# Layer 2 attention: softmax rows scaled on GpSimd ahead of the transposes, with scores two tiles ahead, in place of a widened and transposed reciprocal

## The chip, the cores and the metric

The kernel runs on one core of a Trainium2 chip. It is a chain of four transformer-like layers in one program. The metric is the device time of one execution in microseconds (us), taken as the median of several. Four engines do the computing: TensorE (PE in the rows, its weight loads PEld), VectorE (DVE), ScalarE (ACT) and GpSimd (POOL). Each engine works through its own instructions in order; they wait for each other by semaphores. TensorE writes its results into PSUM, which has eight banks of 128 partitions x 512 float32.

## The reference, cut to what matters

Only the attention of layer 2 is touched. It is called with 8 sequences of 512 rows, 128 wide, and has 16 heads of 64:

```python
q = split_heads(inputs @ Wq)
k = split_heads(inputs @ Wk)
v = split_heads(inputs @ Wv)
scores = jnp.einsum('bnqd,bnkd->bnqk', q, k) + position_bias
attn = jax.nn.softmax(scores, axis=-1)
hidden = jnp.einsum('bnqk,bnkd->bnqd', attn, v)
return hidden @ Wo
```

So each row of exponents must be divided by its sum somewhere between the exponential and the output product.

## The kernel before

`t5_attention_block` works through STEPS = 64 steps, one for each sequence (8) and pair of heads (8). A step n has four tiles t of 128 query rows, and each tile two heads h: eight units of 128 x 512 values. In this text the parts of a step on TensorE have letters:

- **Q, K, V**: the products of the pair (`q_product`, `k_product` into a bank each; `v_product`, four tiles of rows, into the bank of Q). DVE cuts q and k into a high and a low part (`cut_q`, `low_q`, `cut_k`, `low_k`), ACT copies the high ones (`high_q`, `high_k`) and v (`store_v`).
- **S(n,t)** (`scores`, L1690): for a tile, three products for each head, six matmuls of 64 rows, into two PSUM banks, one for each head. There are just these two, so S of the next tile waits for `biased` of this one.
- DVE then adds the bias from the table `skewed` and takes the row's extreme (`bias`, L1868), writing a unit of the ring `p`; ACT raises it in place and sums it (`exponents`, L1797), by `accum_out` into `sums`.
- **T(n,t)** (`turns`, a helper at L129): eight 128 x 128 transposes of the two units of p. DVE and ACT copy one head's result each to `pT` (`move`, L1877 and L1805; the buffer's name is `t_pT` or `g`).
- **M** (`mix`, L1712), in two halves of four matmuls: v times the turned exponents of the step before, a head in each half of the output columns.
- **W** (`turn_scale`, L129): DVE inverts the eight columns of sums of a step (`invert`, L1884), Pool spreads each over 64 columns into `wide` (L1947), PE turns it (four transposes) into the bank of K, ACT copies it to `scale` (L1812), and DVE multiplies the mixed heads by it (`norm`, L1891) into `hT`.
- **O** (`output`, L1727): `wo` times hT, summed over the eight pairs of a sequence in one bank. Once a sequence, `turn_sum` turns the sum back (four transposes; `sum_out` and `store_sum` on DVE).

TensorE's order in a step, written out by hand in the loop over n, is: S(n,1), T0, Q(n+1), K(n+1), S(n,2), T1, first half of M(n-1), S(n,3), T2, second half of M(n-1), S(n+1,0), T3, O(n-2), W(n-1), V(n+1). Scores are thus one tile ahead of the transposes (`after`). The ring p has RING = 4 units. Pool also issues, in the first 32 steps, two indirect DMAs a step (`scatter`, L624), which have nothing to do with the attention but stand behind its instruction on Pool's queue; SP only loads weights of later layers.

Of the kernel before, what the change touches and what calls it, by code (L numbers as in the profile page):

```python
# [19 lines left out]
ALU = mybir.AluOpType  # L20
# [1591 lines left out]
def t5_attention_block(k, wq, wk, wv, wo, skewed, loads, late_loads):  # L1612

    nc, NB = k.nc, k.NB
    PAIRS, HALF, RING = HEADS // 2, P // 2, 4
    STEPS = NB * PAIRS
    with ExitStack() as ctx:
# [9 lines left out]
        wide, scale = st.sb("wide", [P, 8, HALF]), st.sb("scale", [P, SEQ])  # L1627
# [7 lines left out]
        mixed, inverted, widened = st.sem("mixed"), st.sem("inverted"), st.sem("widened")  # L1635
        scale_made, scaled, normed = st.sem("scale_made"), st.sem("scaled"), st.sem("normed")
# [10 lines left out]
        def after(n, t):  # L1647

            return (n, t + 1) if t + 1 < TPS else (n + 1, 0)

        @block.tensor
        def _(pe):
# [7 lines left out]
            def k_product(n):  # L1660
                if n >= 3:
                    pe.wait_ge(scaled, n - 2)
                elif n >= 1:
                    pe.wait_ge(k_low, n)
# [30 lines left out]
            def turns(n, t):  # L1695
                for h in range(2):
                    u = unit(n, t, h)
                    pe.wait_ge(expd, u + 1)
# [17 lines left out]

            def turn_scale(n):
                pe.wait_ge(widened, n + 1)
                pe.wait_ge(k_low, min(n + 3, STEPS))
                turn(nc, kc_ps, [wide[:, 2 * t:2 * t + 2, :].rearrange("p a c -> p (a c)") for t in range(TPS)],  # L1720
                     k.ident).then_inc(scale_made, 1)
# [19 lines left out]
            scores(0, 0)  # L1741
            for n in range(STEPS + 2):
                live = n < STEPS
                if live:
                    scores(n, 1)
                    turns(n, 0)
                if n + 1 < STEPS:
                    q_product(n + 1)
                    k_product(n + 1)
                if live:  # L1750
                    scores(n, 2)
                    turns(n, 1)
# [703 lines left out]
```

## Time and profile before

| what | value |
|---|---|
| median of 3 runs | 2474.96 us (2468.89 to 2475.29) |
| profiled execution, its own time | 2463.91 us |
| its span | 2462.2 us |
| TensorE busy over the span | 2040.5 us (83%) |
| DVE, ACT, POOL busy over the span | 1458.4, 1179.5, 443.8 us |
| the stage in question | from 756.5 to 1751.2 us of the span, 994.7 us |

Rows of a timeline have the start in us, the time from the first start to the last end of what is merged in the row, the engine, the source line, the operation, output <- input, and xN for N instructions merged. TensorE's instructions overlap, so its steps are read from start to start. A float32 matmul of 512 columns is two instructions in the trace (x2), a transpose one. What stands in brackets is idle time of that engine just before, and what ended it. A row of busy times has the stretch, its length, then the busy time of PE, PEld, DVE, ACT and POOL with their instructions, TensorE's granted clock (1.00 is full speed), the busy share of the DMA engines and GB/s.

### The profile page before, as it was taken

The numbers are of one execution on the slowest core, as the hardware profiler recorded it, in microseconds if no ns is written. First come the engines' busy times: TensorE is split into PE (matmuls) and PEld (weight loads), VectorE is DVE, ScalarE is ACT, GpSimd is POOL, SyncE is SP. The second block draws the span as 40 slices with busy tenths as digits, with TensorE's granted clock in tenths as the row PEclk, the third lists the DMA queues.
The fourth block names the chain that finished last, engine by engine and source line by source line (L and its number), as shares of the span: only waits on it lengthen the run. The fifth ranks groups of instructions, "written<-read, shape, count | busy, mean of one in ns | idle before, by whom it ended". The sixth has DMA issues, their size and how long they took to land. (4 is left out here: it accounts for less than half of the span.)

```text
span 2462.2 us, 41326 instructions
## 1 busy us (share of the span) xinstructions
PE 2040.5 (83%) x14039; PEld 1319.4 (54%) x14039; DVE 1458.4 (59%) x4086; ACT 1179.5 (48%) x2380; POOL 443.8 (18%) x522
## 2 busy tenths in 40 slices
PE   3435998468759999999999999999796188989978
PEld 3223996347744555555555555555596034444447
DVE  4675223642166777777777777777464766666615
ACT  1122553234436666666666666666232205555563
POOL 0154551044410111111110000000065100000000
PEclk9866998768959999999999999999898558898899
DMA  3412662045460000000000000001175322322101
GB/s 128 130 41 92 230 228 81 9 136 179 153 172 20 10 10 10 10 10 10 10 6 1 1 1 1 1 1 53 61 254 175 102 71 83 104 66 76 51 4 35
DMA packets 120234, 173.06 MB, mean 70 GB/s; under 512 B 16136, under 2 KB 79344, under 8 KB 119584
## 3 DMA queue, kind: packets, MB, share of 16 engines
q1 hardware_dynamic: 108016, 141.38, 18.2%
q0 software_dynamic: 11584, 23.91, 2.8%
q10 hardware_dynamic: 432, 5.19, 0.5%
q8 instruction: 113, 1.85, 0.3%
q14 instruction: 89, 0.73, 0.1%
HBM read 68.27 MB, written 45.40 MB: 46 GB/s over the span
## 5 line engine op out<-in xcount | busy, mean ns | idle before, releaser
L1797 ACT ACTIVATE t_p<-t_p,t_low 128x512 f32<-128x512 f32 x512 | 369.3, 721 | 333.4 <-DVE t_low L1868 333.3
L1868 DVE CUSTOM_DVE_ANT_0 t_p<-bank,L_skewed 128x512 f32<-128x512 f32 x512 | 332.6, 687 | 276.8 <-PE bank L1690 276.8
L129 PE MATMUL pair<-ident,t_p 128*128 128x128 f32 x2048 | 279.9, 280 | 0.0
L129 PEld LDWEIGHTS pair<-ident,t_p 128*128 128x128 f32 x2048 | 219.0, 141 | 94.8 <-issue 92.6
L2205 ACT ACTIVATE alibi_p<-pair 128x1024 f32<-128x1024 f32 (+1 forms) x192 | 169.0, 884 | 164.6 <-PE pair L2092 164.4
L2264 DVE CUSTOM_DVE_ANT_0 alibi_junk<-bank,alibi_later 128x512 bf16<-128x512 f32 (+1 forms) x256 | 150.8, 623 | 95.2 <-PE bank L2104 92.8
L1947 POOL COPY t_wide<-t_inverse 128x512 f32<-128x512 f32 x64 | 39.1, 611 | 892.2 <-DVE t_inverse L1884 883.4
L2104 PE MATMUL bank<-alibi_k_aug,alibi_q_aug 32*128 32x512 f32 (+1 forms) x256 | 105.3, 559 | 36.7 <-DMA alibi_k_aug<-aug_k 16.8
L1690 PEld LDWEIGHTS bank<-t_k_hi,t_q_hi 64*128 64x128 f32 x512 | 47.7, 183 | 161.6 <-issue 149.6
L1690 PE MATMUL bank<-t_k_hi,t_q_hi 64*128 64x512 f32 x512 | 127.8, 496 | 3.5 <-DVE t_low L1868 3.2
L1712 PE MATMUL pair<-t_pT,t_v 128*64 128x512 f32 x512 | 123.8, 605 | 1.6 <-DVE t_hT L1891 1.6
L1712 PE MATMUL pair<-g,t_v 128*64 128x512 f32 x512 | 124.0, 605 | 0.0
L2151 PE MATMUL bank<-alibi_p,alibi_v_aug 128*32 128x512 f32 (+3 forms) x1024 | 100.2, 490 | 15.6 <-ACT g L2211 15.6
L1690 PE MATMUL bank<-t_k_lo,t_q_hi 64*128 64x512 f32 x512 | 101.7, 394 | 0.0
L1690 PE MATMUL bank<-t_k_hi,t_q_lo 64*128 64x512 f32 x512 | 100.8, 390 | 0.0
L1797 ACT ACTIVATION_READ_ACCUMULATOR t_p<-t_p,t_low 128x1 f32 x512 | 96.3, 188 | 0.0
L2080 PE MATMUL pair<-alibi_q_aug,alibi_k_aug 32*128 32x384 f32 (+3 forms) x512 | 95.6, 412 | 0.3 <-ACT alibi_p L2205 0.2
L742 PEld LDWEIGHTS pair<-L0moe_w,L0moe_hT 128*128 128x128 f32 x624 | 91.9, 193 | 6.3
L742 PE MATMUL pair<-L0moe_w,L0moe_hT 128*128 128x128 f32 x624 | 95.2, 276 | 0.0
L703 POOL DMA_INDIRECT answers<-L0moe_y,L0moe_at x78 | 75.5, 967 | 81.9 <-DVE L0moe_at L803 68.3
L1877 DVE COPY t_pT<-pair 128x512 f32<-128x512 f32 x128 | 87.8, 686 | 1.6 <-PE pair L129 1.6
L2080 PEld LDWEIGHTS pair<-alibi_q_aug,alibi_k_aug 32*128 32x128 f32 x512 | 49.2, 201 | 72.6 <-issue 37.3
(488 smaller groups left out, 4401.6 us busy)
## 6 DMA issues: line engine op xcount, KB each, us to landing
L0moe_w<-L_packed SPq DMA_DIRECT2D x39, 578.0 KB, 3.4
L2moe_w<-L_skewed SPq DMA_DIRECT2D x39, 450.0 KB, 3.1
L1moe_w<-L_packed SPq DMA_DIRECT2D x23, 578.0 KB, 3.4
alibi_q_aug<-aug_q SPq DMA_DIRECT2D x8, 1024.0 KB, 7.6
alibi_k_aug<-aug_k SPq DMA_DIRECT2D x8, 1024.0 KB, 8.1
L_skewed<-bias_table SPq DMA_DIRECT2D x16, 448.0 KB, 10.3
slots<-g ACTq DMA_DIRECT2D x3, 1690.0 KB, 11.9
L0moe_xs<-slots SPq DMA_DIRECT2D x39, 130.0 KB, 3.2
```

Of the source, the lines that this page charges most:

```text
L129: last = nc.tensor.transpose(out[0:piece.shape[1], j * P:j * P + piece.shape[0]], piece, ident[0:piece.shape[0], 0:piece.shape[0]])
L742: ins = nc.tensor.matmul(down_ps[i % 2][:, h * P:(h + 1) * P], hT[:, n % (2 * chunks), h * P:(h + 1) * P], w[:, i % DEEP, at:at + P], star ...
L1690: ins = nc.tensor.matmul(score_ps[h][:], left[rows[h], n % 2, tile], right[rows[h], n % 2, :], start=(j == 0), stop=(j == 2))
L1712: ins = nc.tensor.matmul(mix_ps[rows[h], :], v[:, n % 2, j, rows[h]], pT[n % 2][:, h, j, :], start=(j == 0), stop=(j == TPS - 1))
L1797: nc.scalar.activation(p[:, u % RING, :], p[:, u % RING, :], ACT.Exp, bias=low[:, u % 16:u % 16 + 1], scale=-1.0, accum_out=sums[:, n % 2, ...
L1868: nc.vector.tensor_tensor_reduce(out=p[:, u % RING, :], in0=score_ps[h][:], in1=skewed[:, (n % PAIRS) * 2 + h, start:start + SEQ], scale=- ...
L1877: nc.vector.tensor_copy(pT[n % 2][:, 0, :, t * P:(t + 1) * P], turn_ps[0][:].rearrange("p (j n) -> p j n", n=P)).then_inc(moved[0], 1)
L2080: nc.tensor.matmul(flip_ps[u % 2][:, r % 2, a:e], k_aug[rows(r), n % AUG, G, c * P:(c + 1) * P], q_aug[rows(r), n % AUG, G, c * P:SEQ], st ...
L2104: nc.tensor.matmul(bank[:, 0:w], q_aug[rows(r), b % AUG, G, t * P:w], k_aug[rows(r), b % AUG, G, 0:w], start=True, stop=True).then_inc(sco ...
L2151: ins = nc.tensor.matmul(mix_ps[rows(r), c * P:SEQ], v_aug[:, n % 2, c, 4 * G + r, :], p[:, slot, r % 2, a:e], start=(c == 0), stop=True, ...
L2205: nc.scalar.activation(p[:, u % P_RING, :, 0:w], flip_ps[u % 2][:, :, 0:w], ACT.Exp).then_inc(expd, 1)
L2264: nc.vector.tensor_tensor_reduce(out=junk[:, s % 2, 0:w], in0=score_ps[s % 2][:, 0:w], in1=later[:, SEQ - w:SEQ], scale=1.0, scalar=-HUGE, ...
```

## The change

Pool now multiplies every unit of p in place by one over its row sums, between the exponential and the transposes. DVE inverts two columns of sums a tile in place of eight a step. W, the widened tile, `scale`, its copy on ACT and the multiplication on DVE are gone; what is left of `norm` is a plain copy from PSUM to hT, on ACT. Transposes wait for `divided` in place of `expd`. To leave room for this the scores run two tiles ahead of the transposes, p has 6 units, and the orders on PE, ACT and DVE are written anew. The diff, cut to its core:

```diff
-    PAIRS, HALF, RING = HEADS // 2, P // 2, 4
+    PAIRS, HALF, RING = HEADS // 2, P // 2, 6
...
-            return (n, t + 1) if t + 1 < TPS else (n + 1, 0)
+            return (n, t + 2) if t + 2 < TPS else (n + 1, t + 2 - TPS)
...
             def k_product(n):
-                if n >= 3:
-                    pe.wait_ge(scaled, n - 2)
-                elif n >= 1:
+                if n >= 1:
                     pe.wait_ge(k_low, n)
...
-                    pe.wait_ge(expd, u + 1)
+                    pe.wait_ge(divided, u + 1)
...
-            def turn_scale(n):
-                pe.wait_ge(widened, n + 1)
-                pe.wait_ge(k_low, min(n + 3, STEPS))
-                turn(nc, kc_ps, [wide[:, 2 * t:2 * t + 2, :].rearrange("p a c -> p (a c)") for t in range(TPS)],
-                     k.ident).then_inc(scale_made, 1)
...
+            k_product(1)
+            scores(0, 1)
             for n in range(STEPS + 2):
-                live = n < STEPS
-                if live:
-                    scores(n, 1)
-                    turns(n, 0)
-                if n + 1 < STEPS:
-                    q_product(n + 1)
-                    k_product(n + 1)
+                live, more = n < STEPS, n + 1 < STEPS
                 if live:
                     scores(n, 2)
+                    turns(n, 0)
+                if more:
+                    q_product(n + 1)
+                if live:
+                    scores(n, 3)
                     turns(n, 1)
                 if 1 <= n <= STEPS:
                     mix(n - 1, 0)
                 if live:
-                    scores(n, 3)
                     turns(n, 2)
+                if 1 <= n <= STEPS:
+                    mix(n - 1, 1)
                 if n % PAIRS == 2 and n >= PAIRS and n < STEPS:
                     turn_sum(n // PAIRS - 1)
-                if 1 <= n <= STEPS:
-                    mix(n - 1, 1)
-                if n + 1 < STEPS:
+                if more:
                     scores(n + 1, 0)
                 if live:
                     turns(n, 3)
                 if n >= 2:
                     output(n - 2)
-                if 1 <= n <= STEPS:
-                    turn_scale(n - 1)
-                if n + 1 < STEPS:
+                if more:
+                    scores(n + 1, 1)
                     v_product(n + 1)
+                if n + 2 < STEPS:
+                    k_product(n + 2)
...
-            def store_scale(n):
-                act.wait_ge(scale_made, n + 1)
+            def norm(n):
+                act.wait_ge(mixed, n + 1)
                 if n >= 1:
-                    act.wait_ge(normed, n)
-                nc.scalar.copy(scale[:], kc_ps[:]).then_inc(scaled, 1)
+                    act.wait_ge(added, n)
+                nc.scalar.copy(hT[:], mix_ps[:]).then_inc(normed, 1)
...
-            def invert(n):
-                dve.wait_ge(expd, (n + 1) * 8)
+            def invert(n, t):
+                dve.wait_ge(expd, unit(n, t, 1) + 1)
                 if n >= 2:
-                    dve.wait_ge(widened, n - 1)
-                nc.vector.reciprocal(inverse[:, n % 2, :], sums[:, n % 2, :]).then_inc(inverted, 1)
-
-            def norm(n):
-                dve.wait_ge(mixed, n + 1)
-                dve.wait_ge(scaled, n + 1)
-                if n >= 1:
-                    dve.wait_ge(added, n)
-                nc.vector.tensor_tensor(hT[:], mix_ps[:], scale[:], ALU.mult).then_inc(normed, 1)
+                    dve.wait_ge(divided, unit(n - 1, 0, 0))
+                nc.vector.reciprocal(inverse[:, n % 2, 2 * t:2 * t + 2], sums[:, n % 2, 2 * t:2 * t + 2]).then_inc(inverted, 1)
...
         @block.gpsimd
-                pool.wait_ge(inverted, n + 1)
-                if n >= 1:
-                    pool.wait_ge(scale_made, n)
-                nc.gpsimd.tensor_copy(wide[:], inverse[:, n % 2, :].unsqueeze(2).to_broadcast([P, 8, HALF])).then_inc(widened, 1)
+                for t in range(TPS):
+                    for h in range(2):
+                        u = unit(n, t, h)
+                        pool.wait_ge(inverted, n * TPS + t + 1)
+                        nc.gpsimd.tensor_scalar(p[:, u % RING, :], p[:, u % RING, :], inverse[:, n % 2, t * 2 + h:t * 2 + h + 1],
+                                                None, ALU.mult).then_inc(divided, 1)
```

ACT's order in a step is now, with E for an exponential and its tile of step n: E(2) of head 0, move(0), E(2) of head 1, norm(n-2), high_k(n+1); E(3), move(1), E(3), high_q(n+1); move(2), E and E of tile 0 of step n+1; move(3), E and E of tile 1 of step n+1, store_v(n+1).

TensorE at the end of a step, before; the rows are T(n,3), O, W, V, then S(n+1,1) in three rows and T(n+1,0):

```order
L129 MATMUL pair<-ident,t_p 128x128 x8
L1727 MATMUL pair<-t_hT,L_wo 128x512
L129 MATMUL bank<-ident,t_wide 128x128 x4
L1676 MATMUL bank<-L_wv,xnT 128x128 x4
L1690 MATMUL bank<-t_k_hi,t_q_hi 128x512 x2
L1690 MATMUL bank<-t_k_lo,t_q_hi 128x512 x2
L1690 MATMUL bank<-t_k_hi,t_q_lo 128x512 x2
L129 MATMUL pair<-ident,t_p 128x128 x8
```

The same place now (S is L1686, V L1672, K L1663, O L1717):

```order
L129 MATMUL pair<-ident,t_p 128x128 x8
L1717 MATMUL pair<-t_hT,L_wo 128x512
L1686 MATMUL bank<-t_k_hi,t_q_hi 128x512 x2
L1686 MATMUL bank<-t_k_lo,t_q_hi 128x512 x2
L1686 MATMUL bank<-t_k_hi,t_q_lo 128x512 x2
L1672 MATMUL bank<-L_wv,xnT 128x128 x4
L1663 MATMUL bank<-xnT,L_wk 128x512
```

W is gone, S(n+1,1) stands ahead of V, and K has come here from its place beside Q.

DVE at the start of a step, before. The two rows `ISA` are one `bias`, its main part and the read of its accumulator; then come `move`, the reciprocal, q's two parts and `norm`:

```order
L1868 ISA t_p,t_low<-bank,L_skewed 128x512
L1868 ISA t_low 128x1
L1877 COPY t_pT<-pair 128x4x128
L1884 RECIPROCAL t_inverse<-t_sums 128x8
L1842 TENSOR_SCALAR t_q_cut<-bank 128x512
L1849 TENSOR_TENSOR t_q_lo<-bank,t_q_cut 128x512
L1891 TENSOR_TENSOR t_hT<-pair,t_scale 128x512
L1868 ISA t_p,t_low<-bank,L_skewed 128x512
```

And now, from the reciprocal of tile 1 to that of tile 2:

```order
L1880 RECIPROCAL t_inverse<-t_sums 128x2
L1864 ISA t_p,t_low<-bank,L_skewed 128x512
L1864 ISA t_low 128x1
L1864 ISA t_p,t_low<-bank,L_skewed 128x512
L1864 ISA t_low 128x1
L1873 COPY g<-pair 128x4x128
L1851 TENSOR_SCALAR t_k_cut<-bank 128x512
L1856 TENSOR_TENSOR t_k_lo<-bank,t_k_cut 128x512
L1880 RECIPROCAL t_inverse<-t_sums 128x2
```

A reciprocal, which waits for ACT's exponentials, now stands ahead of each pair of `bias` instructions (or, in the second half of a step, ahead of the `move` in front of them), and `norm` has left the engine.

## Rows read from the trace of the kernel before

**Rows 1.** Busy time of the engines in the stage of layer 2's attention

```profile
756.50:1751.20 994.70, 985.97 (x5792) 560.44 (x5792) 701.17 (x1680) 646.10 (x1536) 101.52 (x128) 1.00 0.03 10
```

**Rows 2.** TensorE's largest wait from 756 to 1745 us: total, times, longest

```profile
PE bank L1690 <- DVE t_low L1868: 3.2, 4, 1.4
```

**Rows 3.** Timeline of TensorE through one step: W, V, S, T, Q, K, S, T, M, S, O, W

```profile
1203.09 0.60 PE L129 MATMUL bank<-ident,t_wide 128*128 128x128 f32 x4
1203.53 1.06 PE L1676 MATMUL bank<-L_wv,xnT 128*128 128x128 f32 x8
1204.51 0.51 PE L1690 MATMUL bank<-t_k_hi,t_q_hi 64*128 64x512 f32 x2
...
1205.42 1.09 PE L129 MATMUL pair<-ident,t_p 128*128 128x128 f32 x8
1206.35 1.02 PE L1658 MATMUL bank<-xnT,L_wq 128*128 128x512 f32 x2
1207.21 1.02 PE L1667 MATMUL bank<-xnT,L_wk 128*128 128x512 f32 x2
1208.16 0.50 PE L1690 MATMUL bank<-t_k_hi,t_q_hi 64*128 64x512 f32 x2
...
1209.05 1.09 PE L129 MATMUL pair<-ident,t_p 128*128 128x128 f32 x8
1210.08 1.94 PE L1712 MATMUL pair<-g,t_v 128*64 128x512 f32 x8
1211.94 0.50 PE L1690 MATMUL bank<-t_k_hi,t_q_hi 64*128 64x512 f32 x2
...
1217.55 1.02 PE L1727 MATMUL pair<-t_hT,L_wo 128*128 128x512 f32 x2
1218.41 0.60 PE L129 MATMUL bank<-ident,t_wide 128*128 128x128 f32 x4
```

**Rows 4.** Timeline at the stage's start, where the engines wait for each other

```profile
761.59 0.69 DVE L1868 CUSTOM_DVE_ANT_0 t_p<-bank,L_skewed 128x512 f32<-128x512 f32 x1 [1.15 <-PE bank L1690]
...
762.21 0.69 DVE L1868 CUSTOM_DVE_ANT_0 t_p<-bank,L_skewed 128x512 f32<-128x512 f32 x1
762.33 0.72 ACT L1797 ACTIVATE t_p<-t_p,t_low 128x512 f32<-128x512 f32 x1 [1.37 <-DVE t_low L1868]
...
762.96 0.19 ACT L1797 ACTIVATION_READ_ACCUMULATOR t_p<-t_p,t_low 128x1 f32 x1
...
762.96 0.50 PE L1690 MATMUL bank<-t_k_hi,t_q_hi 64*128 64x512 f32 x2 [1.38 <-DVE t_low L1868]
763.05 0.71 ACT L1797 ACTIVATE t_p<-t_p,t_low 128x512 f32<-128x512 f32 x1
...
763.97 0.69 DVE L1868 CUSTOM_DVE_ANT_0 t_p<-bank,L_skewed 128x512 f32<-128x512 f32 x1 [1.06 <-PE bank L1690]
```

**Rows 5.** Timeline of the reciprocal and of Pool in the same step

```profile
1207.35 0.19 DVE L1884 RECIPROCAL t_inverse<-t_sums 128x8 f32<-128x8 f32 x1
...
1207.46 0.64 DVE L1842 TENSOR_SCALAR t_q_cut<-bank 128x512 int32<-128x512 int32 x1
...
1207.61 0.61 POOL L1947 COPY t_wide<-t_inverse 128x512 f32<-128x512 f32 x1 [12.31 <-DVE t_inverse L1884]
...
1208.38 0.97 POOL L624 DMA_INDIRECT slots<-s,slot  x1 [0.16 <-issue]
```

**Rows 6.** Timeline in layer 3, where Pool and DVE work at once

```profile
2088.87 1.28 POOL L2352 TENSOR_TENSOR alibi_lo<-alibi_full,alibi_hi 128x512 f32<-128x512 f32 x1 [3.85 <-DVE alibi_hi L2300]
...
2089.15 0.69 DVE L2264 CUSTOM_DVE_ANT_0 alibi_junk<-bank,alibi_later 128x512 bf16<-128x512 f32 x1 [0.36 <-PE bank L2104]
```

**Rows 7.** Timeline at the stage's end: the last M, O, W, and O

```profile
1741.29 3.65 PE L1712 MATMUL pair<-t_pT,t_v 128*64 128x512 f32 x16 [1.55 <-DVE t_hT L1891]
...
1744.87 1.13 PE L1727 MATMUL pair<-t_hT,L_wo 128*128 128x512 f32 x2
...
1747.89 1.13 PE L1727 MATMUL pair<-t_hT,L_wo 128*128 128x512 f32 x2 [1.46 <-DVE t_hT L1891]
```

More of the change, by code:

```diff
@@ L1626, in t5_attention_block @@
         low, sums, inverse = st.sb("low", [P, 16]), st.sb("sums", [P, 2, 8]), st.sb("inverse", [P, 2, 8])
-        wide, scale = st.sb("wide", [P, 8, HALF]), st.sb("scale", [P, SEQ])
         hT, sT = st.sb("hT", [P, SEQ]), st.sb("sT", [P, SEQ])
@@ L1634, in t5_attention_block @@
         moved = [st.sem("moved0"), st.sem("moved1")]
-        mixed, inverted, widened = st.sem("mixed"), st.sem("inverted"), st.sem("widened")
-        scale_made, scaled, normed = st.sem("scale_made"), st.sem("scaled"), st.sem("normed")
+        mixed, inverted, divided, normed = st.sem("mixed"), st.sem("inverted"), st.sem("divided"), st.sem("normed")
         sent = st.sem("sent")
@@ L1795, in exponents @@
                 if t == 0 and h == 0 and n >= 2:
-                    act.wait_ge(inverted, n - 1)
+                    act.wait_ge(inverted, (n - 1) * TPS)
                 nc.scalar.activation(p[:, u % RING, :], p[:, u % RING, :], ACT.Exp, bias=low[:, u % 16:u % 16 + 1], scale=-1.0,
@@ L1816, in _ @@
             store_v(0)
-            exponents(0, 0, 0)
-            exponents(0, 0, 1)
-            for n in range(STEPS + 1):
+            for t in range(2):
+                exponents(0, t, 0)
+                exponents(0, t, 1)
+            for n in range(STEPS + 2):
                 for t in range(TPS):
@@ L1822, in _ @@
                         m, s = after(n, t)
+                        if t >= 2:
+                            move(n, t)
                         if m < STEPS:
                             exponents(m, s, 0)
-                        move(n, t)
+                        if t < 2:
+                            move(n, t)
                         if m < STEPS:
                             exponents(m, s, 1)
+                    if t == 0 and n >= 2:
+                        norm(n - 2)
+                    if t == 0 and n + 1 < STEPS:
+                        high_k(n + 1)
                     if t == 1 and n + 1 < STEPS:
                         high_q(n + 1)
-                        high_k(n + 1)
-                    if t == 3 and n >= 1:
-                        store_scale(n - 1)
                     if t == 3 and n + 1 < STEPS:
@@ L1907, in _ @@
             low_k(0)
-            bias(0, 0, 0)
-            bias(0, 0, 1)
-            for n in range(STEPS + 2):
-                for t in range(TPS):
-                    if n < STEPS:
-                        m, s = after(n, t)
-                        if m < STEPS:
-                            bias(m, s, 0)
-                            bias(m, s, 1)
-                        move(n, t)
-                    if t == 0 and 1 <= n <= STEPS:
-                        invert(n - 1)
+            for t in range(2):
+                bias(0, t, 0)
+                bias(0, t, 1)
+            invert(0, 0)
+            for n in range(STEPS):
+                for t in range(TPS):
+                    m, s = after(n, t)
+                    if t + 1 < TPS:
+                        invert(n, t + 1)
+                    elif n + 1 < STEPS:
+                        invert(n + 1, 0)
+                    if t >= 2:
+                        move(n, t)
+                    if m < STEPS:
+                        bias(m, s, 0)
+                        bias(m, s, 1)
+                    if t < 2:
+                        move(n, t)
                     if t == 0 and n + 1 < STEPS:
+                        cut_k(n + 1)
+                        low_k(n + 1)
+                    if t == 1 and n + 1 < STEPS:
                         cut_q(n + 1)
                         low_q(n + 1)
-                    if t == 0 and n >= 2:
-                        norm(n - 2)
-                    if t == 1 and n + 1 < STEPS:
-                        cut_k(n + 1)
-                        low_k(n + 1)
                     if t == 1 and n % PAIRS == 2 and PAIRS <= n < STEPS:
```

## The prediction, made before the changed kernel ran

> **What bounds the kernel now.** I read the stage's busy times first. In the 994.7 us of layer 2's attention TensorE counts 985.97 us as busy, at a granted clock of 1.00 (its 2.4 GHz level), DVE 701 us, ACT 646 us, Pool 102 us [rows 1]. A busy PE is not PE at its peak, so I then read its waits: over the whole stage the largest sum is 3.2 us, in four waits for DVE at the start [rows 2], and there is one of 1.55 us ahead of the last M [rows 7]. Between those, no semaphore holds it. So a step lasts as long as TensorE's own list, and the third view says how long that is: from W to W it is 1218.41 - 1203.09 = 15.32 us [rows 3]. Read from start to start, its parts are W 0.44, V 0.98, S 0.91, T 0.93 ahead of Q, Q 0.86, K 0.95 ahead of S, T 1.03 ahead of M, half of M 1.86, O 0.86 [rows 3]. The three parts of the step left out of the rows (two S with T, one M) repeat these within 0.02.
>
> The same rows show a cost that belongs to an order and not to an operation: Q followed by K takes 0.86, K followed by S 0.95; T ahead of Q 0.93, ahead of M 1.03 [rows 3]. Going between whole-array matmuls and the half-array ones (S in rows, M in columns) costs 0.09 or 0.10 us.
>
> **The change on TensorE.** Removed: W, 0.44 a step. Moved: S(n+1,1) stands behind O, and S(n,3) behind Q. O costs 0.86 ahead of W and Q 0.86 ahead of K; each is now followed by S, which I price like K ahead of S, 0.95: +0.09 twice. V now leads into K and not into S; by its eight instructions at W's pace (four in 0.44) it should take between 0.88 and 0.98, I take 0.92: -0.06. K ahead of S stays. One half of M now leads into T and not into S; both are changes of the array's division, so I leave it at 1.86. S ahead of V I price like S ahead of T, no difference. Sum: -0.44 + 0.09 + 0.09 - 0.06 = -0.32, a step of 15.00 us. The bounds from rows are -0.26 (V stays at 0.98) and -0.44 (no cost for the new borders).
>
> **The change on the other engines**, and whether it fits under 15.00. Put time 0 at S(n,2). TensorE, if nothing holds it: T0 0.90, Q 1.83, S(n,3) 2.78, T1 3.68, M 4.7, T2 6.57, M 7.6, S(n+1,0) 9.5, T3 10.4, O 11.3, S(n+1,1) 12.25, V 13.15, K 14.1, S(n+1,2) 15.0. What the engines need between each other I take from the start of the stage, where they do wait:
> - S start to bias of head 0: 763.97 - 762.96 = 1.01; bias to bias 762.21 - 761.59 = 0.62; second bias to the next S 762.96 - 762.21 = 0.75 [rows 4].
> - bias to its exponential 0.74; exponential to exponential 0.72; the sum is out at 762.96 + 0.19, 0.82 after the exponential's start, so about 0.88 until DVE can go on [rows 4].
> - reciprocal to the next DVE instruction 0.11, reciprocal to Pool's start 0.26, Pool's copy of 512 columns to its next instruction 0.77 [rows 5].
>
> **The tightest chain** runs from S(n+1,0) to S(n+1,2). Its bias ends only after 1.01 + 0.74 + 0.72 + 0.88 have brought the second exponential's sum to DVE: there the new reciprocal stands in the queue ahead of the move and of the bias of tile 1, and S(n+1,2) is behind that bias. 1.01 + 0.74 + 0.72 + 0.88 + 0.11 (reciprocal) + 0.62 (move) + 0.62 + 0.75 = 5.45 us. TensorE's list between the two is 15.0 - 9.5 = 5.5. It fits with some 0.1 to spare. The other reciprocals have more room: that of tile 2 comes at 4.15 (behind cut_k and low_k), delays the bias of tile 3 to 4.3, and the next S needs that only at 9.5. DVE's work itself is a wash: norm, as wide as a bias (0.69, rows 4), against three more reciprocals of 0.19 [rows 5]. So is ACT's: a copy of PSUM for a copy of PSUM, and at 4.2 it frees M at 4.7.
>
> **Pool's multiplication** has no row. From below it is bounded by the copy of the same width, one input, 0.61 long and 0.77 to the next [rows 5]; from above by the two-input subtraction of 128x512, 1.28 [rows 6], with the same 0.16 behind it 1.44. It reads one tensor, so I take it near the copy: 0.65, 0.8 from one to the next. For tile 2, the one with least time, Pool starts at 4.15 + 0.26 = 4.4; heads are done at 5.1 and 5.9, and T2 wants them at 6.57 and 7.03. At 1.44 the second is done at 7.13 plus a semaphore: up to 0.2 late. The scatter's two DMAs (0.97 each, some 2.5 us together) stand behind tile 3's multiplications: Pool is free of them at about 7.7 + 1.6 + 2.5 = 11.8, and tile 0's reciprocal comes at 12.8. Eight multiplications at 0.8 are 6.4 us of 15. All of this is hidden at 0.8; if that cover went, each 0.1 us by which T is late costs 6.4 us in all.
>
> **The ends.** At the start, K and V of the next step stand in front of T and Pool adds its latency to the first ones: I put +1 us. At the end, the last M waited 1.55 us for hT, and the last O came at 1747.89, 3.0 us after the M made way for the O ahead of it at 1744.87, through W, the scale's copy and norm [rows 7]. Now the M needs only a plain copy that stands right behind the last move, so I take that wait as gone; and from M to the last O there is one ACT copy beside the O ahead of it (0.86), some 0.9 in place of 3.0: -3.7. Together -2.7.
>
> **Sum.** 63 steps x -0.32 = -20.2, with the ends -22.9 us. The profiled execution took 2463.91, so it would be 2441.0; the median of the runs shown is 11 us above that execution, and the same difference gives 2474.96 - 22.9 = 2452. By the bounds: -0.26 a step gives 2456, -0.44 (where the DVE chain of 5.45 would bind too, within 0.1) 2445 or a little less; Pool at 1.44 gives back 0.2 a step, 2465.
>
> **Rivals.**
> 1. *Part of the gain goes to new waits* (0.17). Either Pool costs nearly what the two-input row says, or the chain of 5.45 is longer than I add up by 0.1 to 0.3, since it has only 0.1 to spare: 0.2 a step given back is 2465, 0.3 is 2471. For it speaks that this chain crosses four engines and that in the kernel before DVE's bias never stood behind ACT's sums. Against it: every link has a row.
> 2. *Pool and DVE block each other* (0.10), the case on the slower side. Pool reads and writes 512 columns eight times a step while DVE runs. If in the tight chain one DVE instruction had to wait out one multiplication, 0.65 more would make it 6.1 against TensorE's 5.5: +0.55 a step, less 0.32, is +14 us, with the ends 2487; two such blocks would make it 2528. It turns slower than before once the chain is some 0.45 longer. Against it: in layer 3, Pool's subtraction (1.28, two reads) overlaps a DVE instruction of just the kind of `bias`, one input in PSUM, one in SBUF, and that takes the 0.69 that it takes alone [rows 4, 6].
>    The Trainium skill, "SBUF — State Buffer", in the rules on the port pair that DVE and GpSimd share, has this very rule: whichever starts first holds the pair for its whole instruction when the DVE instruction is in a 2-port mode or has two SBUF inputs. By its other half, an instruction with at most one SBUF input does not contend, this chain's DVE work would be free of it, and the trace agrees (0.69 in both places).
> 3. *Nothing is gained* (0.03): W filled time in which TensorE would have waited anyway. Its few microseconds of waits in the whole stage [rows 2, 7] leave no room for that. 2472.
>
> **How the numbers follow.** Forecast 0.70, 2452 us, its own range 2442 to 2459. A measurement of this kernel can tell about 0.3% (7.4 us) from no change, so faster is below 2467.5: the forecast and 0.12 of rival 1, 0.82. Within 0.3%: 0.05 of rival 1 and rival 3, 0.08. Slower: rival 2, 0.10. The range runs from 2441 (no cost for the new borders, and the spread of the runs) to 2468, which takes in Pool's upper bound and leaves out rival 2 and the worse part of rival 1.
>
> **What the profile would show.** TensorE's list from S to S at 15.0 us with next to no waits; Q and O ahead of S at 0.95, V ahead of K near 0.92. Pool's rows at 0.6 to 0.8 us, 512 of them; if they are at 1.3, T waits for Pool by up to 0.2. S(n+1,2) waiting for DVE a step means that the chain of 5.45 is mis-added. A bias that takes more than 0.69 while Pool runs means rival 2. An end of the stage with under 1 us between the last M and the last O. I am wrong if TensorE shows a wait in every step, wherever it is.

## The result, and the profile after

The changed kernel takes 2501.57 us, the median of 4 runs (2497.41 to 2503.7), against 2475.12 us (4 runs, 2468.89 to 2475.99) for the kernel before beside it: a ratio of 1.0126, 95% interval 1.0106 to 1.0145. It is slower by 26.5 us, where 23 us less were forecast. The profiled execution took 2500.13 us.

First the page of the changed kernel, its costliest groups: line, engine, operation, output <- input, count | busy us, mean ns of one | idle time before, and what ended it.

```profile
L1941 POOL TENSOR_SCALAR t_p<-t_p,t_inverse 128x512 f32<-128x512 f32 x512 | 793.1, 1562 | 163.5 <-DVE t_inverse L1880 157.9
...
L1864 DVE CUSTOM_DVE_ANT_0 t_p<-bank,L_skewed 128x512 f32<-128x512 f32 x512 | 331.4, 685 | 197.9 <-PE bank L1686 197.9
L129 PE MATMUL pair<-ident,t_p 128*128 128x128 f32 x2048 | 299.1, 283 | 22.3 <-POOL t_p L1941 21.1
L129 PEld LDWEIGHTS pair<-ident,t_p 128*128 128x128 f32 x2048 | 217.0, 141 | 165.8 <-POOL t_p L1941 110.8
```

Pool's multiplication takes 1562 ns, not 650. And TensorE's transposes, which had no wait worth a row [rows 2], now have one, for Pool. The waits of TensorE over the same 756 to 1745 us as [rows 2], total, times, longest:

```profile
PE pair L129 <- POOL t_p L1941: 20.3, 64, 0.9
PE bank L1686 <- DVE t_low L1864: 2.1, 3, 1.4
```

64 times in 20.3 us is about once a step, 0.32 us in the mean. Where in the step, the timeline of TensorE shows; these rows answer to [rows 3] (S is L1686, Q L1656, M L1708, O L1717, V L1672, K L1663):

```profile
1002.25 0.50 PE L1686 MATMUL bank<-t_k_hi,t_q_hi 64*128 64x512 f32 x2
...
1003.14 1.09 PE L129 MATMUL pair<-ident,t_p 128*128 128x128 f32 x8
1004.07 1.02 PE L1656 MATMUL bank<-xnT,L_wq 128*128 128x512 f32 x2
1005.02 0.50 PE L1686 MATMUL bank<-t_k_hi,t_q_hi 64*128 64x512 f32 x2
...
1005.92 1.16 PE L129 MATMUL pair<-ident,t_p 128*128 128x128 f32 x8
1007.01 1.94 PE L1708 MATMUL pair<-g,t_v 128*64 128x512 f32 x8
1008.88 0.66 PE L129 MATMUL pair<-ident,t_p 128*128 128x128 f32 x4
1009.80 0.66 PE L129 MATMUL pair<-ident,t_p 128*128 128x128 f32 x4 [0.27 <-POOL t_p L1941]
1010.39 1.94 PE L1708 MATMUL pair<-g,t_v 128*64 128x512 f32 x8
1012.26 0.50 PE L1686 MATMUL bank<-t_k_hi,t_q_hi 64*128 64x512 f32 x2
...
1014.08 1.02 PE L1717 MATMUL pair<-t_hT,L_wo 128*128 128x512 f32 x2
1015.04 0.50 PE L1686 MATMUL bank<-t_k_hi,t_q_hi 64*128 64x512 f32 x2
...
1015.93 1.16 PE L1672 MATMUL bank<-L_wv,xnT 128*128 128x128 f32 x8
1016.92 1.02 PE L1663 MATMUL bank<-xnT,L_wk 128*128 128x512 f32 x2
1017.88 0.50 PE L1686 MATMUL bank<-t_k_hi,t_q_hi 64*128 64x512 f32 x2
```

A step is 1017.88 - 1002.25 = 15.63 us (15.64 between other O's), against 15.32 before. T2 is split: from its first head to M it takes 10.39 - 8.88 = 1.51 us, where an undisturbed T takes 1.03 ahead of M [rows 3]. T1 is stretched a little: 1.09 to M. The rest is as forecast within 0.02, save one: V ahead of K takes 0.99, not 0.92. Pool beside it:

```profile
1006.40 0.15 DVE L1880 RECIPROCAL t_inverse<-t_sums 128x2 f32<-128x2 f32 x1
...
1006.65 6.31 POOL L1941 TENSOR_SCALAR t_p<-t_p,t_inverse 128x512 f32<-128x512 f32 x4 [0.28 <-DVE t_inverse L1880]
```

Tile 2's reciprocal comes at 1006.40 and Pool starts 0.25 later, 4.40 us after S(n,2): just the 4.4 of the prediction. Four multiplications, the two of tile 2 and the two of tile 3, then take 6.31 us, (6.31 - 1.56) / 3 = 1.58 from one to the next. The second head's is done at 1006.65 + 1.58 + 1.56 = 1009.79, and the transposes of that head start at 1009.80.

How long the stage is, one row per kernel tells: the instructions of O, with the shortest, median and longest in ns and the first and last start in us. For the kernel before:

```profile
L1727 PE MATMUL pair<-t_hT,L_wo x128: 592/594/697, 802.5 to 1748.4; 128*128 128x512 f32 x128
```

And after:

```profile
L1717 PE MATMUL pair<-t_hT,L_wo x128: 592/594/697, 810.2 to 1775.4; 128*128 128x512 f32 x128
```

The last O comes 27.0 us later, in a stage that began at nearly the same time (756.3 and 756.5): about as much as the 26.5 us between the medians. 7.7 of it are there at the first O. From the last O to the end of the span it is 723.0 us after and 713.8 before; over the kernels of this study this part is 711.4 to 723.0, though nothing in it was changed. It goes with the clock that TensorE was granted there: 0.81 of full speed in the three profiles with 720.6 to 723.0 (the changed kernel, experiments 4 and 5), 0.82 or 0.83 in the nine with 711.4 to 715.9. Why the clock differs is open. Below I therefore compare the last O's as well as the times.

### The profile page after: what moved, and what is told of

It reads as the page before. It is cut to its first block and busy times, and to the rows that moved or that the text cites. A ratio compares the mean times of both kernels' runs of the same rounds, so it can differ in the third digit from the quotient of the medians.

```text
span 2498.4 us, 41381 instructions
## 1 busy us (share of the span) xinstructions
PE 2059.6 (82%) x13783; PEld 1284.0 (51%) x13783; DVE 1440.0 (58%) x4214; ACT 1178.9 (47%) x2380; POOL 1192.7 (48%) x970
## 5 line engine op out<-in xcount | busy, mean ns | idle before, releaser
L1941 POOL TENSOR_SCALAR t_p<-t_p,t_inverse 128x512 f32<-128x512 f32 x512 | 793.1, 1562 | 163.5 <-DVE t_inverse L1880 157.9
L129 PE MATMUL pair<-ident,t_p 128*128 128x128 f32 x2048 | 299.1, 283 | 22.3 <-POOL t_p L1941 21.1
L2347 POOL TENSOR_TENSOR alibi_lo<-alibi_full,alibi_hi 128x512 f32<-128x512 f32 x16 | 20.3, 1270 | 362.3 <-DVE alibi_hi L2295 339.2
L1686 PEld LDWEIGHTS bank<-t_k_hi,t_q_hi 64*128 64x128 f32 x512 | 47.8, 183 | 193.7 <-DVE t_low L1864 144.5
L1686 PE MATMUL bank<-t_k_hi,t_q_hi 64*128 64x512 f32 x512 | 127.8, 496 | 3.6 <-DVE t_low L1864 3.0
L1708 PE MATMUL pair<-t_pT,t_v 128*64 128x512 f32 x512 | 123.8, 605 | 1.1 <-ACT t_hT L1803 1.1
L1708 PE MATMUL pair<-g,t_v 128*64 128x512 f32 x512 | 124.0, 605 | 0.0
L703 POOL DMA_INDIRECT answers<-L0moe_y,L0moe_at x78 | 74.7, 957 | 81.6 <-DVE L0moe_at L803 68.0
L1880 DVE RECIPROCAL t_inverse<-t_sums 128x2 f32<-128x2 f32 x256 | 41.0, 160 | 122.7 <-ACT t_p L1788 122.7
L624 POOL DMA_INDIRECT slots<-L_rows,slot x64 | 65.6, 1026 | 93.3 <-POOLq L1114 47.4
L1686 PE MATMUL bank<-t_k_lo,t_q_hi 64*128 64x512 f32 x512 | 101.3, 392 | 0.0
L1686 PE MATMUL bank<-t_k_hi,t_q_lo 64*128 64x512 f32 x512 | 101.1, 391 | 0.0
L703 POOL DMA_INDIRECT answers<-L2moe_y,L2moe_at x78 | 74.8, 958 | 48.2 <-DVE L2moe_at L803 34.3
```

Of the source, the lines that this page charges most:

```text
L129: last = nc.tensor.transpose(out[0:piece.shape[1], j * P:j * P + piece.shape[0]], piece, ident[0:piece.shape[0], 0:piece.shape[0]])
L703: nc.gpsimd.indirect_dma_start(out=k.answers, out_offset=bass.IndirectOffsetOnAxis(at[:, i % AT_DEEP, h:h + 1], 0), in_=y[:, i % Y_DEEP, h ...
L1686: ins = nc.tensor.matmul(score_ps[h][:], left[rows[h], n % 2, tile], right[rows[h], n % 2, :], start=(j == 0), stop=(j == 2))
L1708: ins = nc.tensor.matmul(mix_ps[rows[h], :], v[:, n % 2, j, rows[h]], pT[n % 2][:, h, j, :], start=(j == 0), stop=(j == TPS - 1))
L1941: nc.gpsimd.tensor_scalar(p[:, u % RING, :], p[:, u % RING, :], inverse[:, n % 2, t * 2 + h:t * 2 + h + 1], None, ALU.mult).then_inc(divid ...
```

## The experiments

Theory A: Pool's multiplication costs 1.56, T2 and T1 come late by that, and nothing else is wrong. Theory B: the new order of TensorE, with its chain of 5.45 us over four engines, costs more than I added up, whatever Pool does. Theory C: Pool and DVE hold each other up.

**1. The new order, without the multiplications.** All eight are left out (so the division by the sums is missing), and T waits for the exponentials:

```diff
-                    pe.wait_ge(divided, u + 1)
+                    pe.wait_ge(expd, u + 1)
...
-                if n >= 2:
-                    dve.wait_ge(divided, unit(n - 1, 0, 0))
...
-                for t in range(TPS):
-                    for h in range(2):
-                        u = unit(n, t, h)
-                        pool.wait_ge(inverted, n * TPS + t + 1)
-                        nc.gpsimd.tensor_scalar(p[:, u % RING, :], p[:, u % RING, :], inverse[:, n % 2, t * 2 + h:t * 2 + h + 1],
-                                                None, ALU.mult).then_inc(divided, 1)
+                pool.wait_ge(inverted, (n + 1) * TPS)
```

> The changed kernel with Pool's multiplications left out (the rows of p are not divided by their sums) and the transposes waiting for the exponentials; orders on all engines as changed. Theory (price): the changed step lasts 15.64 us because one multiplication on Pool costs 1.55 us, so that the second head of tile 2 comes 0.47 us late and the first 0.06. Without it a step is 15.1, the stage some 34 us shorter, about 2467 us. Rival (order): the new order and the reciprocals in DVE's queue cost the time whatever Pool does; then the step stays at 15.5 or more and the time near 2500.

Measured: 2450.57 us (4 runs, 2438.04 to 2454.74), ratio to before 0.9891 (0.9842 to 0.9940); last O at 1733.7. Two O's in a row on its timeline of TensorE:

```profile
1439.51 1.02 PE L1717 MATMUL pair<-t_hT,L_wo 128*128 128x512 f32 x2
...
1454.58 1.02 PE L1717 MATMUL pair<-t_hT,L_wo 128*128 128x512 f32 x2
```

15.07 us a step. The time is some 16 us below the expected 2467: the first O comes 6.7 us sooner than in the changed kernel, and the part behind the last O is 10 us shorter, at the higher clock. The order by itself gains 0.25 and has no wait of its own: over 800 to 1720 us TensorE waits for nothing longer than 0.5 us, twice. Theory B falls. Pool's work is worth 15.64 - 15.07 = 0.57 us a step.

**2. The removal alone.** The kernel before in its old order, without W, its copy and its multiplication (the division is missing here too; `norm` is a plain copy on DVE):

```diff
-                if 1 <= n <= STEPS:
-                    turn_scale(n - 1)
...
-                nc.vector.tensor_tensor(hT[:], mix_ps[:], scale[:], ALU.mult).then_inc(normed, 1)
+                nc.vector.tensor_copy(hT[:], mix_ps[:]).then_inc(normed, 1)
```

> The kernel before with W left out (the four transposes of the widened reciprocals, the copy to scale, and the multiplication by it, so nothing is divided by the sums), norm a plain copy on DVE; all other orders as before. It measures by itself what taking W away is worth on TensorE. Both theories: 0.44 us a step less, or 0.35 if the border between O and V costs something, so 14.9 and about 2445 us. If W had been hidden, no change from 2475.

Measured: 2437.74 us (4 runs), ratio 0.9860 (0.9817 to 0.9903), last O at 1716.3, and a step (from one O to the next, 1441.51 to 1456.39) of 14.88 us. W was worth 15.32 - 14.88 = 0.44, all of it. The old order without W is 0.19 a step shorter than the new one without its multiplications: that is what Q and O ahead of S cost (0.09 each), and 0.01 for V ahead of K.

**3. The same multiplication as another instruction.** Pool multiplies with `tensor_tensor`, the column of 1/sum spread along the row by its access pattern. The result and the order are the same:

```diff
-                        nc.gpsimd.tensor_scalar(p[:, u % RING, :], p[:, u % RING, :], inverse[:, n % 2, t * 2 + h:t * 2 + h + 1],
-                                                None, ALU.mult).then_inc(divided, 1)
+                        row = inverse[:, n % 2, t * 2 + h:t * 2 + h + 1].to_broadcast([P, SEQ])
+                        nc.gpsimd.tensor_tensor(p[:, u % RING, :], p[:, u % RING, :], row, ALU.mult).then_inc(divided, 1)
```

> The changed kernel with Pool multiplying by a tensor-tensor instruction whose second input is the column of the reciprocal, broadcast over 512 columns. Theory (price): that form should cost about 1.27 us like the subtraction in layer 3; two of them are 0.56 us less, more than the 0.47 by which tile 2 is late, so T2 waits no more and the step is 15.1 to 15.2, about 2468 us. If the form costs 1.55 too, or the order is to blame, 2500.

Measured: 2447.42 us (6 runs, 2444.31 to 2463.16), ratio 0.9905 (0.9870 to 0.9939); last O at 1734.1, 0.4 us from that of experiment 1. The first row is from its groups of instructions, the second is all there is of waits of TensorE from 800 to 1720 us:

```profile
L1942 POOL TENSOR_TENSOR t_p<-t_p,t_inverse 128x512 f32<-128x512 f32 x512 | 521.8, 1041 | 394.3 <-DVE t_inverse L1880 394.3
```

```profile
PE bank L1686 <- DVE t_low L1864: 0.9, 2, 0.5
```

At 1.04 us Pool is hidden wholly: from O to O 15.07 us, as without any multiplication. The chain of four engines, the reciprocals and Pool's place in it are all still there, and only the instruction's form is another. That settles A for nearly the whole of the loss: one number of one instruction turned a gain of some 1% into a loss of 1.3%.

**4. The prices on Pool apart.** In the kernel before, from step 36 on where Pool is nearly idle, it runs pairs of multiplications on a tile that nobody uses, each waiting for the one ahead; 8 of each kind.

```diff
+                elif n >= 36:
+                    for _ in range(2):
+                        count[0] += 1
+                        pool.wait_ge(probed, count[0])
+                        probe((n - 36) // 4)
```

> The kernel before, with extra instructions on Pool's queue in steps 36 to 63, where it is idle for 14 us a step: two of a kind in each step, four steps a kind, on a tile of their own of 128x512 float32: multiply by a scalar column, by an immediate, tensor by tensor, tensor by a broadcast column, copy of a broadcast column, and by a scalar column on 256 and on 128 columns. It measures the disputed cost by itself. Theory (price): scalar column 1.55, broadcast column 1.02, tensor by tensor 1.27, copy 0.61, whatever the other engines do; if the 1.55 came from the load of the scalar it would be a constant, and 128 columns would cost over 1 us; if it is the pace, 256 columns cost 0.8 and 128 columns 0.45. Rival (contention with DVE or in place): 1.0 or less here.

Its groups on Pool; `eps` is a column of one value, spread along the row in the `TENSOR_TENSOR` and the `COPY`:

```profile
L1949 POOL TENSOR_SCALAR t_pa<-t_pa,eps 128x512 f32<-128x512 f32 x8 | 12.5, 1566 | 0.4
L1951 POOL TENSOR_SCALAR t_pa<-t_pa 128x512 f32<-128x512 f32 x8 | 11.9, 1489 | 0.3
L1955 POOL TENSOR_TENSOR t_pa<-t_pa,eps 128x512 f32<-128x512 f32 x8 | 8.3, 1040 | 0.3
L1953 POOL TENSOR_TENSOR t_pa<-t_pa 128x512 f32<-128x512 f32 x8 | 8.3, 1040 | 0.3
L1959 POOL TENSOR_SCALAR t_pa<-t_pa,eps 128x256 f32<-128x256 f32 x8 | 7.4, 923 | 0.4
L1957 POOL COPY t_pa<-eps 128x512 f32<-128x512 f32 x8 | 4.9, 614 | 0.2
L1961 POOL TENSOR_SCALAR t_pa<-t_pa,eps 128x128 f32<-128x128 f32 x8 | 4.8, 602 | 0.4
```

Among these it is the operation's kind that sets the price, and not the number of inputs: `tensor_scalar` costs 1.57 with a column, 1.49 with a constant, `tensor_tensor` 1.04, where I had expected 1.27 for two tensors. From 128 to 512 columns it grows by (1566 - 602) / 384 = 2.51 ns a column, with some 0.28 us besides. It costs here what it costs in the changed kernel (1.566 and 1.562). DVE works beside it in both, so this pair by itself does not clear DVE; the trace of the changed kernel does. In the step shown above DVE stands still from 1010.35 to 1013.26, and the multiplication that runs from 1011.40 to 1012.96 takes 1.56 all the same.

**5. Another place for T2.** Both halves of M ahead of T2, which gives T2 1.87 us more of room and saves one border between M and T:

```diff
                 if 1 <= n <= STEPS:
                     mix(n - 1, 0)
+                    mix(n - 1, 1)
                 if live:
                     turns(n, 2)
-                if 1 <= n <= STEPS:
-                    mix(n - 1, 1)
```

> The changed kernel with both halves of M ahead of T2 in TensorE's order, nothing else. Theory (price): T2 comes 1.9 us later and finds its rows ready although Pool still takes 1.55; and two borders between M and T fall away, 0.2 to 0.26 us. A step without scatter is 14.9. In the 32 steps with scatter Pool itself has 8 x 1.55 + 2.7 us and its waits of some 0.3 to 0.7, so 15.1 to 15.7 there. Together about 2465 us (2455 to 2480). Rival (order): no gain beyond the borders, some 2485.

Measured: 2456.97 us (7 runs), ratio 0.9945 (0.9911 to 0.9978), last O at 1740.9. With Pool still at 1.56, steps take 15.06 once the scatters are over (O at 1446.04 and 1461.10), and by turns some 15.06 and 15.21 with them. That is 0.58 a step saved with Pool's price unchanged; 0.15 of it is the border of M that is gone (experiment 6), so the room for T2 gave 0.43. Without the scatters T3 is now the one that Pool makes a little late (1.07 to O in place of 0.93), since its two multiplications stand right behind those of tile 2 on Pool; with them it is T1, 1.16 and 1.28 to M in two steps in a row, in place of 1.03.

**6. Both edits**, 3 and 5, in one kernel.

> The changed kernel with both edits: Pool multiplies by the tensor-tensor form with the broadcast column (1.02 us one, as the run before showed) and both halves of M stand ahead of T2. Theory (price, and borders of TensorE's order): with the cheap form no T waits, 15.07 a step; M in one piece saves the two borders between M and T, 0.26 us by this kernel's rows, so 14.81 a step and some 17 us less than the cheap form alone, about 2431 us. Rival: another wait stands right behind (the chain from S(n+1,0) to S(n+1,2) of 5.45, or T3), and the step stays near 15.0, 2444.

Measured: 2439.33 us (6 runs, 2435.79 to 2446.14), ratio 0.9879 (0.9845 to 0.9913), last O at 1723.0.

```profile
1446.47 1.02 PE L1717 MATMUL pair<-t_hT,L_wo 128*128 128x512 f32 x2
...
1461.39 1.02 PE L1717 MATMUL pair<-t_hT,L_wo 128*128 128x512 f32 x2
```

14.92 us a step, 0.15 under experiment 3: M in one run of 16 takes 3.59 instead of twice 1.87, which saves 0.15, and T ahead of S costs the 1.02 that T ahead of M does; for that reason the step is not the 14.81 that I had expected, for which both borders had to go. This version computes what the reference does and beats both kernels.

**7. Only tile 2 with the cheap form**, to split the 0.57 by tile:

```diff
-                        nc.gpsimd.tensor_scalar(p[:, u % RING, :], p[:, u % RING, :], inverse[:, n % 2, t * 2 + h:t * 2 + h + 1],
-                                                None, ALU.mult).then_inc(divided, 1)
+                        col = inverse[:, n % 2, t * 2 + h:t * 2 + h + 1]
+                        if t == 2:
+                            ins = nc.gpsimd.tensor_tensor(p[:, u % RING, :], p[:, u % RING, :], col.to_broadcast([P, SEQ]), ALU.mult)
+                        else:
+                            ins = nc.gpsimd.tensor_scalar(p[:, u % RING, :], p[:, u % RING, :], col, None, ALU.mult)
+                        ins.then_inc(divided, 1)
```

> The changed kernel with the cheap form (tensor by broadcast column, 1.04 us) for the two units of tile 2 alone; the six others stay at 1.56. It tells tile 2's lateness from Pool's load. Theory (lateness of tile 2): nearly the whole gain of the cheap form comes back, 15.1 a step, about 2450 us. Rival (Pool's load as a whole, with scatter in 32 steps): only the 1.04 us of load goes, so the steps with scatter stay at 15.4 or more, 2465 or more.

Measured: 2464.04 us (10 runs), ratio 0.9972 (0.9953 to 0.9992); last O at 1741.2. Steps take 15.12 without the scatters (1445.29, 1460.41) and by turns some 15.14 and 15.28 with them. Tile 2 is thus 0.52 of the 0.57 where Pool has nothing else to do; with the scatters in front of tile 0, T1 comes late as well (1.23 to M in one step), at 1.56 a multiplication. The time lies between the two that I had expected: lateness of tile 2 is most of the loss, Pool's load a small part in 32 of the steps.

**8. All multiplications on DVE**, where one costs 0.48, to see whether another engine would do better. `divide` stands behind the two `bias` of its quarter of the step:

```diff
...
                     if m < STEPS:
                         bias(m, s, 0)
                         bias(m, s, 1)
+                    if t == 0:
+                        divide(n, 1)
                     if t < 2:
                         move(n, t)
+                    if t == 1:
+                        divide(n, 2)
+                    if t == 2:
+                        divide(n, 3)
+                    if t == 3 and n + 1 < STEPS:
+                        divide(n + 1, 0)
...
```

> The changed kernel with all the multiplications on DVE (a tensor by scalar column, in place, SBUF to SBUF) behind the bias instructions, Pool left with its scatter. Theory (price): DVE should do one in 0.42 us, as it does the cut of 128x512 in SBUF in layer 3, 0.35 to the next, 2.8 us a step on an engine that has 4 us to spare; T2's first head comes some 0.3 us late, so a step of 15.1 to 15.4, 2450 to 2465 us. Rival: DVE becomes the bound, 15.7 or more, 2500.

Measured: 2657.41 us (4 runs), ratio 1.0762 (1.0714 to 1.0809): much slower, against my expectation. Its timeline at one place:

```profile
1400.55 0.69 DVE L1865 CUSTOM_DVE_ANT_0 t_p<-bank,L_skewed 128x512 f32<-128x512 f32 x1 [1.55 <-PE bank L1687]
...
1401.78 0.88 DVE L1888 TENSOR_SCALAR t_p<-t_p,t_inverse 128x512 f32<-128x512 f32 x2
...
1402.32 1.09 PE L129 MATMUL pair<-ident,t_p 128*128 128x128 f32 x8 [1.80 <-DVE t_p L1888]
```

DVE itself waits 1.55 us for a score, S(n+1,0); behind that bias stands the multiplication of tile 3, for which T3 waits 1.80. DVE has the time, but the queue has the wrong thing at its head. Something comes on top: in some steps TensorE's clock falls after that wait. T3 and O in such a step:

```profile
1474.89 1.71 PE L129 MATMUL pair<-ident,t_p 128*128 128x128 f32 x8 [1.80 <-DVE t_p L1888]
1476.39 1.92 PE L1718 MATMUL pair<-t_hT,L_wo 128*128 128x512 f32 x2
```

O takes 1.92 in place of 1.02, and the granted clock from 1475.5 to 1477.5 is 0.50, the 1.2 GHz level. Steps at full clock take 17.74, those with such a fall up to 19.2 (19.7 where `turn_sum` stands in the step as well).

**9. The same, with tile 3's multiplications ahead of that bias:**

```diff
                     if t >= 2:
                         move(n, t)
+                    if t == 2:
+                        divide(n, 3)
                     if m < STEPS:
...
-                    if t == 2:
-                        divide(n, 3)
```

> The run with all multiplications on DVE, with one edit: those of tile 3 stand ahead of the bias of the next step's tile 0 in DVE's queue, no longer behind it. There T3 waited 1.8 us in every step, since that bias waits for scores which TensorE issues just ahead of T3. Theory (the place in the queue was to blame, not DVE's load): that wait goes, T2's 0.6 us stay, so a step of 15.3 to 15.8, 2460 to 2500 us. Rival (DVE is full: some 13.5 us of a 15 us step): it stays over 16.5 a step, above 2550.

Measured: 2507.17 us (4 runs), ratio 1.0144 (1.0106 to 1.0181), last O at 1785.1, a step 15.87. That is 150 us below experiment 8, and T3 waits no more. Not all of the 150 is the place in the queue itself. The last O comes 158 us sooner: 9 are there at the first O, 60 steps at 17.74 - 15.87 = 1.87 make 112, and the other 37 go with the clock, whose mean from the first O to the last is 0.97 in experiment 8 and 1.00 here. The step is a little over the 15.3 to 15.8 that I had expected. What is left is mainly T2, once a step; T1 comes 0.17 late besides, with no row of its own:

```profile
1455.56 1.09 PE L129 MATMUL pair<-ident,t_p 128*128 128x128 f32 x8 [0.58 <-DVE t_p L1888]
```

So DVE in this order is no better place than Pool at 1.56, and worse than Pool at 1.04. Whether still another order would do wasn't tried.

**10. One head on each engine**, to let Pool and DVE run at once on instructions with both operands in SBUF (theory C's case): head 1 as in experiment 8, head 0 on Pool.

> The changed kernel with head 1 multiplied on DVE and head 0 on Pool by the instruction as changed, so that both engines read and write p in SBUF at once. It tells whether the two block each other. If they do, the DVE instruction that falls into one of Pool's 1.55 us takes more than its 0.42, up to 1.9, and the step is over 15.4; if not, it takes 0.42 always, and T waits for nothing: 15.1 a step, 2448 us.

Measured: 2548.99 us (4 runs), ratio 1.0332 (1.0287 to 1.0377). It inherits the queue of experiment 8, so its time says nothing of C. The two kinds of multiplication seldom overlap either, only at the start of the stage and at its end. The start:

```profile
762.93 0.49 DVE L1888 TENSOR_SCALAR t_p<-t_p,t_inverse 128x512 f32<-128x512 f32 x1
...
762.99 3.41 POOL L1958 TENSOR_SCALAR t_p<-t_p,t_inverse 128x512 f32<-128x512 f32 x2 [32.03 <-DVE t_inverse L1882]
...
765.10 0.71 DVE L1888 TENSOR_SCALAR t_p<-t_p,t_inverse 128x512 f32<-128x512 f32 x1
```

Here two multiplications of Pool take 3.41 rather than 3.1, and one of DVE 0.71 rather than 0.48. At the end two more of DVE, each begun while one of Pool runs, take 0.76 and 0.87 (starts 1811.73 and 1817.39), while Pool's stay at 1.56. All of them in this kernel, with shortest, median and longest ns:

```profile
L1888 DVE TENSOR_SCALAR t_p<-t_p,t_inverse x256: 475/481/866, 762.9 to 1817.4; 128x512 f32<-128x512 f32 x128
L1958 POOL TENSOR_SCALAR t_p<-t_p,t_inverse x256: 1555/1563/1867, 763.0 to 1816.4; 128x512 f32<-128x512 f32 x128
```

Something holds, by 0.2 to 0.4 us, instructions that both work in SBUF. DVE's at 765.10 did not wait for the end of Pool's, which had 1.3 us to go; the others leave that open. For the change itself it doesn't matter, as its DVE instructions show:

```profile
L1864 DVE CUSTOM_DVE_ANT_0 t_p<-bank,L_skewed x512: 668/686/694, 761.4 to 1760.7; 128x512 f32<-128x512 f32 x171
...
L1941 POOL TENSOR_SCALAR t_p<-t_p,t_inverse x512: 1552/1562/1577, 765.2 to 1765.1; 128x512 f32<-128x512 f32 x171
```

These are two lines of code of the changed kernel. Pool is busy for 857 of the stage's 1022 us, and not one bias of 512 took over 694 ns. Theory C falls for this kernel.

## Why the prediction was wrong, point by point

**The step that failed** is the price of Pool's multiplication: "It reads one tensor, so I take it near the copy: 0.65, 0.8 from one to the next", bounded from above by the two-input subtraction at 1.28. It takes 1.56, and 1.58 from one to the next: 2.4 times the value taken, and above the upper bound. Two things were wrong in it. I ordered the instructions by the number of their inputs, and took the row of another operation for a ceiling; experiment 4 shows that the one with fewer inputs is the dearer. And between ends a factor of two apart I chose the one that made the whole plan fit, with no row that spoke for it beyond "one input".

The Trainium skill, "GPSIMD Engine Reference", section 3.1, would have led the same way: it puts the best case at some 1.8 cycles an element, 769 ns measured for 512 elements, and two-input work at 2.6 cycles, as the two-input floor. No run here shows the 769 ns; the order measured here is the reverse of what I would have taken from it (1.56 for `tensor_scalar` with one tensor, 1.04 for `tensor_tensor`), and the measurement decides.

**What followed from it** went by the prediction's own frame. Pool's start at 4.4 was right (4.40). With 1.58 and 1.56 the second head is done at 7.54 and T2 wanted it at 7.03: 0.5 late, and T2 took 0.49 more than undisturbed, T1 0.06. The sum is 15.07 + 0.55 = 15.62, measured 15.64. Rival 1 named this mechanism and its place, but with 0.2 a step, because its price was bounded by the same row.

**TensorE's list.** W -0.44: right, by experiment 2. Q and O ahead of S +0.09 each: right (0.95 and 0.96). One half of M leading into T, 1.86: right (1.87). V ahead of K -0.06: wrong, it takes 0.99 and not 0.92; V's eight instructions don't run at W's pace, and leading into K saves nothing. So the list is -0.25, the pessimistic bound of the sum, and 15.07 where 15.00 was forecast (experiments 1 and 3). The sum left out one border: seven times the step holds `turn_sum`, which now stands between M and S and costs 0.59 (15.66 - 15.07 in experiment 1) where it cost 0.44 (15.76 - 15.32), 1 us in all.

**The tightest chain**, 5.45 us from S(n+1,0) to S(n+1,2), held. In the step shown the second `bias` of tile 1 starts at 1016.83, and with the 0.75 from there to the next S the chain is 1016.83 - 1012.26 + 0.75 = 5.32. TensorE's list between the two is 1017.88 - 1012.26 = 5.62, mostly since V takes 0.99, and S shows no wait there.

**The ends.** Forecast +1 and -3.7, measured +7.7 at the first O and -1.6 in the two waits that the forecast named. The start is Pool's price again: with the cheap form the first O is at 803.9, +1.4. At the end three rows answer to [rows 7]:

```profile
1769.40 3.65 PE L1708 MATMUL pair<-t_pT,t_v 128*64 128x512 f32 x16 [1.12 <-ACT t_hT L1803]
1772.98 1.12 PE L1717 MATMUL pair<-t_hT,L_wo 128*128 128x512 f32 x2
1774.84 1.12 PE L1717 MATMUL pair<-t_hT,L_wo 128*128 128x512 f32 x2 [0.73 <-ACT t_hT L1803]
```

The wait of M for hT did not go, 1.12 in place of 1.55, and from O to the last O it is 1.86, not 0.9. What both copies to hT on ACT waited for, total, times, longest:

```profile
ACT t_hT L1803 <- PE pair L1717: 5.6, 2, 4.9
```

They waited for O, not for M: `norm` stands behind `act.wait_ge(added, n)`, since it overwrites the hT that the O ahead still reads. The last M ends at 1773.05, the O ahead at 1774.10, and the copy starts at 1774.20. O, copy, O is serial, as O, copy, M is, and I had put the copy beside the O ahead of it. Together -1.6 in place of -3.7.

**Rival 2** (Pool and DVE block each other) had the sign of the result and not its cause: `bias` takes 0.685 in the mean beside a Pool busy for 84% of the stage. This agrees with the rule of the Trainium skill, "SBUF — State Buffer", section "Who interferes with whom", that a DVE instruction with at most one input in SBUF, outside the 2-port modes, doesn't contend with GpSimd. **Rival 3** is refuted by experiment 2.

**Adding up**, on the last O: 53 steps x 0.32 (15.64 - 15.32) and the seven with `turn_sum` x 0.46 (16.22 - 15.76) make 20, and with 7.7 at the start, less 0.7 between the O's of the last three steps, 27; measured 27.0. With the cheap form the last O is 14.3 us earlier than before. By the ratio, its time is 23.5 us below that of before beside it, with an interval of 15 to 32; what lies beyond the 14.3 is within the interval or outside the stage, and these runs don't tell which.

## What to carry to other kernels

Don't bound an instruction that the trace doesn't show by the number of its inputs or by the row of another operation on the same engine; when the whole plan hangs on it, work out at which price the plan breaks (here some 1.3 us, two of them between Pool's start at 4.4 and T2's second head at 7.03) and make the forecast as wide as both sides of that. When an engine is asked to feed the one that bounds the kernel, count when each result is wanted and not the busy share: Pool at 84% of the stage was hidden, but for 0.06 us, at three tiles of four, and moving other work in front of the fourth gave back most of what a faster instruction did (0.43 of 0.57). Where the bounding engine needs a result, don't queue the work for it behind an instruction that itself waits for that engine: here it cost 1.87 us a step.

## What the runs showed of the hardware

- On Pool, `tensor_scalar` on 128x512 float32 takes 1.56 us (1.49 with a constant), `tensor_tensor` 1.04 with one tensor twice or with a broadcast column, and the copy of a broadcast column 0.61. The subtraction of [rows 6], two separate tensors, has 1.28: why it lies above 1.04 is open.
- The same `tensor_scalar` in place on DVE takes 0.48 us (experiment 8).
- Leaving T for S costs TensorE what leaving T for M does, 1.02 (experiment 6) against 0.93 to whole-array work: M and S both use half of the array.
- Multiplications of Pool and DVE that both have their operands in SBUF delayed each other by 0.2 to 0.4 us in the four cases where they met (experiment 10). Four are too few to say by what rule.
- TensorE's granted clock fell to its 1.2 GHz level in some steps of experiment 8, behind waits of 1.80 us; every step there has one of these and one of 0.58. With a single wait of 0.58 (experiment 9) or 1.2 us (experiment 10) in every step its mean from the first O to the last was 1.00.
